# Transposing attention probabilities by 64x64 matmuls in the four quarters of the array

## The chip, the cores and the metric

The kernel runs on one core of one Trainium2 chip. Its metric is the device time of one execution in microseconds. Three runs of the kernel before took 2162.98, 2164.35 and 2164.65 us; their median is 2164.35 us.

## The reference

A layer of a graph network over 128 graphs of 64 nodes, with 512 channels, in float32: layer norm, attention with 8 heads of 64 channels inside each graph (only where `adj` allows), an output projection with a residual, a second layer norm and an MLP of width 2048 with a residual. Cut to what matters:

```python
nx = _layernorm(x, ln1_g, ln1_b)
q = (nx @ Wq + bq).reshape(B, S, HEADS, HEAD_DIM)      # B = 128 graphs, S = 64 nodes
k = (nx @ Wk + bk).reshape(B, S, HEADS, HEAD_DIM)
v = (nx @ Wv + bv).reshape(B, S, HEADS, HEAD_DIM)
scores = jnp.einsum('bqhd,bkhd->bhqk', q, k) / np.sqrt(HEAD_DIM)
scores = jnp.where(adj_mask[:, None, :, :], scores, NEG)
attn = jax.nn.softmax(scores, axis=-1)
out = jnp.einsum('bhqk,bkhd->bqhd', attn, v).reshape(B, S, H)
x = x + out @ Wo + bo
nx = _layernorm(x, ln2_g, ln2_b)
return x + jax.nn.gelu(nx @ W1 + b1, approximate=False) @ W2 + b2
```

The last product of the attention sums over the keys, so the probabilities, which come out of the softmax with the queries on the partitions, have to be turned until the keys lie there. That turn is what changes.

## The kernel before

There are 8192 tokens, that is 64 tiles of 128 tokens. A tile holds two graphs: graph a = 0 on partitions 0 to 63 and graph a = 1 on partitions 64 to 127. The attention half of the kernel goes through 16 groups of four tiles; two tiles make a pair, so each group has two pairs u = 0 and u = 1, and t = 0, 1 is the tile in its pair. The MLP half follows and is not touched.

The order of the work on TensorE in one group is a list written out by hand (`ORDER`). Its letters are steps: S the scores of a pair, P the transposition of a pair's probabilities, O the product of probabilities and values ("attend"), W the output projection of a tile, and U one of the twelve units that make queries, keys and values of the group after. The list is S0, U0 to U3, P0, U4, U5, S1, O0, U6, U7, W0, U8, W1, P1, U9, O1, U10, U11, W2, W3. Groups 1 to 12 are a hardware loop of two groups a turn; the last two groups have lists of their own (the last one has late units of the values, L, and first products of the MLP, F, between its steps). Each U and each W is twelve matmuls of 128x512 (lines 181 to 183), because a product is made of three matmuls over split parts, for four blocks of channels.

S and O already consist of 64x64 matmuls of plain float32 operands. A matmul takes rows a of the array (the partitions of its operands) and puts its result on 64 of the 128 output partitions; the innermost loops go round the four quarters. In `attend` (O, line 1361) the graph a selects the rows and also the PSUM bank, and the head's half selects the output partitions.

P is `prob_transposes` (line 1344): eight transposes of 128x128, one for each head. The stationary operand is `prob` of one head, 128 queries (two graphs) by 128 columns (two tiles by 64 keys), and the moving operand is the 128x128 identity `ident`. The result of a head has (tile t, key) on the partitions and (graph a, query) in the columns, in `ps_probT`, which is two PSUM banks of four heads each.

ScalarE then copies it to SBUF in four pieces of 64 partitions by 512 columns (`take_probT`, line 717), one for each t and a, which puts graph a on partitions 64a and up. O waits for these four copies (`probT_done`), and P waits for the softmax's last instruction on VectorE (`prob`, line 977, `prob_done`) and for the four copies of the pair before. VectorE's next `prob` in turn waits until P has read the last (`pt_done`).

Where a wait's value is held in a register, inside the loop, a helper called `wait_apart` waits and then increments a semaphore of its own that nobody waits for.

Of the kernel before, what the change touches and what calls it, by code (L numbers as in the profile page):

```python
# [31 lines left out]
F32 = mybir.dt.float32  # L32
# [6 lines left out]
P = 128  # L39
GRAPHS, NODES, HID = 128, 64, 512  # L40
HEADS = 8
# [111 lines left out]
def bank_of(g, kind, n):  # L153
    return ring_place(g, kind, n)[0]

def wait(eng, sem, value):

    if not isinstance(value, int) or value > 0:
        eng.wait_ge(sem, value)  # L160
# [10 lines left out]
def wait_apart(eng, sem, value, passed):  # L171

    wait(eng, sem, value)
    if not isinstance(value, int):
        eng.sem_inc(passed, 1)
# [9 lines left out]
def adj_layer(nc, x_dram, adj, ln1_g, ln1_b, ln2_g, ln2_b, wq, bq, wk, bk, wv, bv, wo, bo, w1, b1, w2, b2, out_dram):  # L186
# [10 lines left out]
    with ctx:  # L197
# [3 lines left out]
        def sem(name):  # L201
            return ctx.enter_context(nc.semaphore(name))
# [3 lines left out]
        ident = sb("ident", [P, P])  # L206
# [15 lines left out]
        start = nc.sbuf_base  # L222

        with ExitStack() as phase:
# [23 lines left out]
            prob = sb("prob", [P, HEADS, 2, NODES])  # L249
# [39 lines left out]
        with ExitStack() as phase:  # L289
            lin_banks = phase.enter_context(nc.psum_tensor("lin", [P, LIN, GT], F32))  # L290
            lin = [lin_banks[:, i] for i in range(LIN)]
            ps_scores = phase.enter_context(nc.psum_tensor("ps_scores", [P, HEADS, 2, NODES], F32))
            ps_probT = phase.enter_context(nc.psum_tensor("ps_probT", [P, HEADS, P], F32))
        with ExitStack() as phase:
            ps_out = [phase.enter_context(nc.psum_tensor(f"ps_out{i}", [P, HID], F32)) for i in range(TILES)]
            ps_x, ps_z, ps_y, ps_r = (phase.enter_context(nc.psum_tensor(f"ps_{n}", [P, GT], F32)) for n in "xzyr")
# [13 lines left out]
        w_loaded, w_hi_done, w_lo_done = ([sem(f"w{c}_{s}") for c in "qkvo"] for s in ("loaded", "hi_done", "lo_done"))  # L310
        cols_loaded, rows_loaded, mlp_cols_loaded = sem("cols_loaded"), sem("rows_loaded"), sem("mlp_cols_loaded")
        filled, ident_done = sem("filled"), sem("ident_done")
        s_passed, o_passed = sem("s_passed"), sem("o_passed")
        stats_done, moments_done, var_done = sem("stats_done"), sem("moments_done"), sem("var_done")
        rstd_done, zn_done, t_done = sem("rstd_done"), sem("zn_done"), sem("t_done")
        z_transposed = sem("z_transposed")
# [4 lines left out]
        prob_done, pt_done, probT_done = sem("prob_done"), sem("pt_done"), sem("probT_done")  # L321
# [345 lines left out]
        def _(act):  # L667
# [42 lines left out]
            def take_probT(g, u):  # L710

                act.wait_ge(pt_done, PAIRS * g + u + 1)
                wait(act, o_done, PAIRS * g + u)
                for t in range(2):
                    for a in range(2):
                        act.activation(probT[a * NODES:(a + 1) * NODES, t],  # L717
                                       ps_probT[t * NODES:(t + 1) * NODES, :, a * NODES:(a + 1) * NODES],
                                       ACT.Copy).then_inc(probT_done, 1)

            def att_hi(g, u):
# [5 lines left out]
            def body(g, par):  # L727
                def unit(j):
                    if "U" in kinds_of(g):
                        take = take_q if j % 3 == 0 else take_k  # L730
                        take(g + 1, 1 - par, j // 3, bank_of(g, "U", j))
                unit(0)
                exponent(g, 0)
                unit(1)
                unit(3)
                take_probT(g, 0)
                unit(4)
                if g < PREP:
                    job_hi(g, 1)
                att_hi(g, 0)  # L740
                unit(6)
                exponent(g, 1)
                unit(7)
                if g < PREP:
                    job_hi(g, 2)
                take_probT(g, 1)
                unit(9)
                att_hi(g, 1)
                unit(10)
                if "N" in kinds_of(g):  # L750
                    for k in range(KC):
                        affine(g + 2, k)
                    for k in range(KC):
                        nx_hi(g + 2, k)
                for n in ln_tiles(g):
                    ln_tile_affine(n)
# [65 lines left out]
            def last_body(g):  # L822
                for n in range(4):
                    conv_hi(0, n)
                exponent(g, 0)
                take_probT(g, 0)
                exponent(g, 1)
                att_hi(g, 0)
                snap(0, 0)
                for n in range(4, PROD):  # L830
                    conv_hi(0, n)
                take_probT(g, 1)
                att_hi(g, 1)
                snap(0, 1)
# [440 lines left out]
        def _(pe):  # L1275
# [62 lines left out]

            def prob_transposes(g, u):
                n = PAIRS * g + u  # L1340
                pe.wait_ge(prob_done, n + 1)
                wait(pe, probT_done, 4 * n)
                for h in range(HEADS):
                    mm = pe.transpose(ps_probT[:, h, :], prob[:, h, :, :], ident[:, :])  # L1344
                mm.then_inc(pt_done, 1)

            def attend(g, par, u, banks):
# [27 lines left out]
            def body(g, par):  # L1375
                for kind, n in order_of(g):
                    if kind == "S":
                        score(g, par, n)
                    elif kind == "P":
                        prob_transposes(g, n)  # L1380
                    elif kind == "F":
                        product(0, 0, n)
                    elif kind == "L":
                        unit(g, n, take_bank(g, "L", n))
                    elif kind == "U":
                        unit(g + 1, n, take_bank(g, "U", n))
                    elif kind == "O":
                        attend(g, par, n, [take_bank(g, "O", 2 * n + a) for a in range(2)])
                    elif kind == "W":
                        project(g, n, take_bank(g, "W", n))  # L1390
                    else:
                        transposes(g + 2, par, n, take_bank(g, "T", n))
# [75 lines left out]
            for t in range(TILES):  # L1468
                pe.wait_ge(zn_done, t + 1)
                for k in range(KC):  # L1470
                    mm = pe.transpose(lin[bank_of(-2, "T", k)][:, t * P:(t + 1) * P], x[0][:, t, k * P:(k + 1) * P],
                                      ident[:, :])
# [41 lines left out]
```

## Time and profile before

| what | value |
| --- | --- |
| median of three runs | 2164.35 us |
| the profiled execution, its own time | 2164.58 us |
| its span | 2162.7 us |
| TensorE busy | 2127.7 us (98%) |
| VectorE busy | 1487.9 us (69%) |
| ScalarE busy | 905.2 us (42%) |
| GpSimd busy | 433.7 us (20%) |
| mean granted TensorE clock | 0.996 |

The span is the time between the first and last instruction that the profile holds; the execution's own time is 1.9 us longer. Shares of busy time are means over stages: the attention half runs from about 60 to 855 us of the span and the MLP half from there. Times in the timeline are microseconds from the span's start. Matmuls overlap: the time that one costs is read from the start of one to the start of the next, and not from its length.

### The profile page before, as it was taken

The page shows a single profiled execution, that of the slowest core. Times are in us where ns is not written, and L with a number is a line of the kernel's source. Part 1 is how long each engine was busy: PE and PEld are TensorE (multiplying, and loading weights), DVE is VectorE, ACT ScalarE, POOL GpSimd, SP SyncE. Part 2 cuts the span into 40 slices and gives each one's busy share as a digit, 9 for nine tenths or more (in the row PEclk, how much of TensorE's full clock was granted, in tenths as well). Part 3 has the DMA queues.
Part 4 walks back from the last instruction along what each step waited for, and adds up shares of the span by engine and source line. Part 5 has one row for each costly group of instructions (what it writes and reads, how often), then busy time and mean ns, then how long its engine had stood idle before and what let it go on. Part 6 is the DMA issues. An engine that isn't in the chain of part 4 may idle for free.

```text
span 2162.7 us, 33121 instructions
## 1 busy us (share of the span) xinstructions
PE 2127.7 (98%) x13216; PEld 1756.9 (81%) x13216; DVE 1487.9 (69%) x2205; ACT 905.2 (42%) x1318; POOL 433.7 (20%) x291
## 2 busy tenths in 40 slices
PE   7999999999999988999999999999999999999999
PEld 6788888888888876888888888888888888888887
DVE  4888888888999965666666656656666666656433
ACT  3444444443344443345345345345345345345332
POOL 2333433321111114003003003003003103103200
PEclk9999999999999998999999999999999999999999
DMA  4344333331222114444544544544544544544532
GB/s 147 129 153 156 135 133 133 138 124 65 70 75 70 46 50 185 156 180 172 193 180 165 199 180 165 199 174 171 199 167 173 204 160 174 209 153 174 217 126 93
DMA packets 103793, 323.98 MB, mean 150 GB/s; under 512 B 21360, under 2 KB 29552, under 8 KB 87280
## 3 DMA queue, kind: packets, MB, share of 16 engines
q1 hardware_dynamic: 98144, 321.68, 40.4%
q8 instruction: 85, 1.39, 0.3%
q10 hardware_dynamic: 5520, 0.55, 0.2%
q14 instruction: 44, 0.36, 0.0%
HBM read 265.57 MB, written 56.62 MB: 149 GB/s over the span
## 4 chain that ended last, share of the span: by engine, by line
PE 96%; DVE 1%; ACT 1%; POOL 1%; DMA 1%; issue 0%; SPq 0%; ACTq 0%; DVEq 0%; POOLq 0%
PE lin L181 11%; PE lin L182 10%; PE lin L183 10%; PE ps_r L181 5%; PE ps_r L182 5%; PE ps_r L183 5%; PE ps_out L181 5%; PE ps_out L182 5%; PE ps_out L183 5%; PE ps_x L181 5%; PE ps_x L182 5%; PE ps_x L183 5%; PE ps_z L181 3%; PE ps_z L182 3%; PE ps_z L183 3%; PE ps_scores L1334 2%
## 5 line engine op out<-in xcount | busy, mean ns | idle before, releaser
L1168 DVE TENSOR_TENSOR acc<-ps_r,acc 128x512 f32<-128x512 f32 x256 | 176.5, 690 | 327.8 <-PE ps_r L183 327.0
L798 ACT ACTIVATE snaps<-ps_x 128x512 f32<-128x512 f32 x192 | 114.4, 596 | 410.7 <-PE ps_x L183 410.7
L181 PE MATMUL ps_r<-w_ring,h_ring 128*128 128x512 f32 x512 | 199.6, 390 | 0.9 <-DVE h_ring L1158 0.9
L181 PE MATMUL ps_x<-nxc,w_ring 128*128 128x512 f32 x512 | 199.4, 389 | 0.0
L183 PE MATMUL ps_r<-w_ring,h_ring 128*128 128x512 f32 x512 | 199.2, 389 | 0.0
L183 PE MATMUL ps_x<-nxc,w_ring 128*128 128x512 f32 x512 | 199.2, 389 | 0.0
L182 PE MATMUL ps_x<-nxc,w_ring 128*128 128x512 f32 x512 | 199.2, 389 | 0.0
L182 PE MATMUL ps_r<-w_ring,h_ring 128*128 128x512 f32 x512 | 199.2, 389 | 0.0
L181 PE MATMUL ps_out<-w_ring,h_ring 128*128 128x512 f32 x512 | 199.2, 389 | 0.0
L183 PE MATMUL ps_out<-w_ring,h_ring 128*128 128x512 f32 x512 | 199.2, 389 | 0.0
L182 PE MATMUL ps_out<-w_ring,h_ring 128*128 128x512 f32 x512 | 199.2, 389 | 0.0
L542 POOL TENSOR_TENSOR xres<-xres,bo_all 128x512 f32<-128x512 f32 x64 | 87.8, 1383 | 448.6 <-DMA xres<-in_x 444.5
L928 DVE STREAM_TRANSPOSE z1T<-x 32x512 f32<-32x512 f32 x224 | 157.5, 703 | 5.3
L928 DVE STREAM_TRANSPOSE bT<-xb 32x512 f32<-32x512 f32 x224 | 157.4, 703 | 4.3
L807 ACT ACTIVATE hf_a<-hf_a,b_cols 128x512 f32<-128x512 f32 x128 | 92.7, 724 | 150.6 <-DVE hf_a L1153 150.6
L1158 DVE TENSOR_TENSOR h_ring<-hf_b,h_ring 128x512 fp32r<-128x512 f32 x128 | 91.4, 714 | 50.3 <-ACT h_ring L814 50.1
L633 POOL TENSOR_TENSOR rstd<-var_eps,minus_half 128x4 f32<-128x4 f32 x14 | 19.4, 1384 | 500.8 <-DVE var_eps L1124 500.8
L717 ACT ACTIVATE probT<-ps_probT 64x512 f32<-64x512 f32 x128 | 75.9, 593 | 95.2 <-PE ps_probT L1344 92.8
L181 PEld LDWEIGHTS ps_r<-w_ring,h_ring 128*128 128x128 f32 x512 | 96.1, 188 | 22.5 <-issue 2.3
L697 ACT ACTIVATE qT<-lin,cols 128x512 f32<-128x512 f32 x64 | 44.1, 689 | 164.2 <-PE lin L183 164.2
L183 PEld LDWEIGHTS ps_r<-w_ring,h_ring 128*128 128x128 f32 x512 | 96.1, 188 | 20.1
L181 PEld LDWEIGHTS ps_x<-nxc,w_ring 128*128 128x128 f32 x512 | 96.1, 188 | 20.0
(131 smaller groups left out, 5131.1 us busy)
## 6 DMA issues: line engine op xcount, KB each, us to landing
w_ring<-w_scratch SPq DMA_DIRECT2D x64, 1792.0 KB, 7.3
w_ring<-w_scratch SPq DMA_DIRECT2D x64, 1024.0 KB, 7.1
xb<-x_scratch SPq DMA_DIRECT2D x22, 1024.0 KB, 10.2
xres<-in_x SPq DMA_DIRECT2D x64, 256.0 KB, 2.8
x_scratch<-xres SPq DMA_DIRECT2D x64, 256.0 KB, 2.2
x<-in_x SPq DMA_DIRECT2D x15, 1024.0 KB, 6.0
acc<-x_scratch SPq DMA_DIRECT2D x32, 256.0 KB, 2.9
out<-xb SPq DMA_DIRECT2D x32, 256.0 KB, 2.0
```

The costliest lines, as they stand in the source:

```text
L181: pe.matmul(out, lhs[1], rhs[0], start=first, stop=False, skip_group_check=resumed)
L182: pe.matmul(out, lhs[0], rhs[1], start=False, stop=False, skip_group_check=resumed)
L183: return pe.matmul(out, lhs[0], rhs[0], start=False, stop=last, skip_group_check=resumed)
L542: pool.tensor_tensor(xres[:, t % 2], xres[:, t % 2], bo_all[:, :], ALU.add).then_inc(xres_biased, 1)
L697: act.activation(qT[par][:, m, :], lin[bank][:, :], ACT.Identity, bias=cols[:, 2, m:m + 1]).then_inc(q_done, 1)
L717: act.activation(probT[a * NODES:(a + 1) * NODES, t], ps_probT[t * NODES:(t + 1) * NODES, :, a * NODES:(a + 1) * NODES], ACT.Copy).then_in ...
L798: act.activation(snaps[:, j], ps_x[:, :], ACT.Copy).then_inc(snap_done[j], 1)
L807: act.activation(hf[c], ps_x[:, :] if c == "C21" else hf[c], ACT.Gelu, bias=b1_cols[:, m:m + 1]).then_inc(gelu_done[c], 1)
L928: return dve.transpose(to[channels, :, :].rearrange("p k (t n) -> p t k n", n=P)[:, :, :, tokens], source[tokens, :, :].rearrange("p t (k ...
L1158: dve.tensor_tensor(h_ring[:, n % 2, 1, at], hf[c], h_ring[:, n % 2, 0, at].bitcast(F32), ALU.subtract).then_inc(h_split[c], 1)
L1168: dve.tensor_tensor(acc(t), ps_r[:, :], acc(t), ALU.add).then_inc(acc_added, 1)
L1334: mm = pe.matmul(ps_scores[a * NODES:(a + 1) * NODES, h * KC + m, t, :], qT[par][rows, m, at:at + NODES], kT[par][rows, m, at:at + NODES], ...
```

## The change

P becomes 32 plain matmuls of 64x64 for each pair in place of eight transposes of 128x128. For each head, tile t and graph a, the stationary operand is the 64x64 block `prob[graph a, head, tile t]`, the moving operand the 64x64 block of the identity on the same partitions, and the result goes to the output partitions of tile t. The graph selects the array's rows and the PSUM bank, the tile the array's columns. The bank of graph a now holds all eight heads of that graph side by side, so each of ScalarE's four copies reads 512 columns in a row from one bank, where it read eight runs of 64 columns, four in each of two banks. The four copies, what they write, and everything on VectorE, GpSimd and the DMA queues are as before.

The two waits ahead of P change places, and the one for `prob_done` goes through `wait_apart` with a new semaphore `p_passed`.

```diff
-            ps_probT = phase.enter_context(nc.psum_tensor("ps_probT", [P, HEADS, P], F32))
+            ps_probT = phase.enter_context(nc.psum_tensor("ps_probT", [P, 2, HEADS, NODES], F32))
...
-        s_passed, o_passed = sem("s_passed"), sem("o_passed")
+        s_passed, p_passed, o_passed = sem("s_passed"), sem("p_passed"), sem("o_passed")
...
                         act.activation(probT[a * NODES:(a + 1) * NODES, t],
-                                       ps_probT[t * NODES:(t + 1) * NODES, :, a * NODES:(a + 1) * NODES],
+                                       ps_probT[t * NODES:(t + 1) * NODES, a],
                                        ACT.Copy).then_inc(probT_done, 1)
...
                 n = PAIRS * g + u
-                pe.wait_ge(prob_done, n + 1)
                 wait(pe, probT_done, 4 * n)
+                wait_apart(pe, prob_done, n + 1, p_passed)
                 for h in range(HEADS):
-                    mm = pe.transpose(ps_probT[:, h, :], prob[:, h, :, :], ident[:, :])
+                    for t in range(2):
+                        for a in range(2):
+                            rows = slice(a * NODES, (a + 1) * NODES)
+                            mm = pe.matmul(ps_probT[t * NODES:(t + 1) * NODES, a, h, :], prob[rows, h, t, :],
+                                           ident[rows, rows], start=True, stop=True)
                 mm.then_inc(pt_done, 1)
```

On TensorE, inside the loop, P0 stands between U3 (queries' weights `wq`) and U4 (keys' weights `wk`). The rows are instructions in program order, moving operand named first; "x7" is a run of equal instructions, and names in brackets are semaphores waited for.

```order
 L182 MATMUL lin<-nxT_lo,wq_hi 128x512
 L183 MATMUL lin<-nxT_hi,wq_hi 128x512
-L1341 REGISTER_ALU
-L160 REGISTER_ALU [waits prob_done]
-L1344 MATMUL ps_probT<-ident,prob 128x128 [waits probT_done]
-L1344 MATMUL ps_probT<-ident,prob 128x128 x7
+L160 REGISTER_ALU
+L160 REGISTER_ALU [waits probT_done]
+L1347 MATMUL ps_probT<-ident,prob 64x64 [waits prob_done]
+L1347 MATMUL ps_probT<-ident,prob 64x64 x31
 L181 MATMUL lin<-nxT_hi,wk_lo 128x512 [waits q_done]
 L182 MATMUL lin<-nxT_lo,wk_hi 128x512
```

The step keeps its place; 8 matmuls become 32, and the wait on the first of them is now the one for the softmax.

P1, on the same engine in the same loop, stands between W1 (output weights `wo`) and U9, and only U9 lies between it and O1, which needs its result.

```order
 L182 MATMUL lin<-wo_lo,attT_hi 128x512
 L183 MATMUL lin<-wo_hi,attT_hi 128x512
-L1341 REGISTER_ALU
-L1344 MATMUL ps_probT<-ident,prob 128x128 [waits probT_done,prob_done]
-L1344 MATMUL ps_probT<-ident,prob 128x128 x7
+L160 REGISTER_ALU [waits probT_done]
+L1347 MATMUL ps_probT<-ident,prob 64x64 [waits prob_done]
+L1347 MATMUL ps_probT<-ident,prob 64x64 x31
 L181 MATMUL lin<-nxT_hi,wq_lo 128x512 [waits k_done]
 L182 MATMUL lin<-nxT_lo,wq_hi 128x512
```

Here too nothing moves past another step: the neighbours of P1 are the same before and now.

## Rows read from the trace of the kernel before

**Rows 1.** Head of the page: span, busy time of each engine, its share, instructions.

```profile
span 2162.7 us, 33121 instructions
PE 2127.7 (98%) x13216; PEld 1756.9 (81%) x13216; DVE 1487.9 (69%) x2205; ACT 905.2 (42%) x1318; POOL 433.7 (20%) x291
```

**Rows 2.** Busy time by stretch: length, then each engine, PEclk, DMA share, GB/s.

```profile
107.00:760.00 653.00, 652.88 (x6002) 539.49 (x5994) 563.26 (x831) 279.28 (x398) 179.60 (x139) 1.00 0.31 108
```

**Rows 3.** Timeline of TensorE: start, length, engine, line, operation, count; P1, later O1.

```profile
140.56 0.39 PE L183 MATMUL lin<-wo_hi,attT_hi 128*128 128x512 f32 x1
140.79 1.03 PE L1344 MATMUL ps_probT<-ident,prob 128*128 128x128 f32 x8
...
141.90 0.40 PE L182 MATMUL lin<-nxT_lo,wq_hi 128*128 128x512 f32 x1
...
144.18 0.39 PE L183 MATMUL lin<-nxT_hi,wq_hi 128*128 128x512 f32 x1
144.50 1.16 PE L1361 MATMUL lin<-probT,v 64*64 64x64 f32 x64
...
145.93 0.39 PE L182 MATMUL lin<-nxT_lo,wk_hi 128*128 128x512 f32 x1
```

**Rows 4.** The same timeline around S0 of a group in the loop.

```profile
206.70 0.39 PE L183 MATMUL lin<-wo_hi,attT_hi 128*128 128x512 f32 x1
207.02 1.16 PE L1334 MATMUL ps_scores<-kT,qT 64*64 64x64 f32 x64
...
208.45 0.39 PE L182 MATMUL lin<-nxT_lo,wq_hi 128*128 128x512 f32 x1
```

**Rows 5.** One line's instructions: records, ns minimum/median/maximum, starts, forms; S, O, P.

```profile
L1334 PE MATMUL ps_scores<-kT,qT x2048: 218/218/365, 54.3 to 821.1; 64*64 64x64 f32 x187
...
L1361 PE MATMUL lin<-probT,v x2048: 218/218/268, 75.7 to 848.3; 64*64 64x64 f32 x187
...
L1344 PE MATMUL ps_probT<-ident,prob x256: 270/272/477, 68.3 to 844.4; 128*128 128x128 f32 x128
```

**Rows 6.** Timeline of ScalarE's copies after P1, then O1 and its copy.

```profile
242.51 2.44 ACT L717 ACTIVATE probT<-ps_probT 64x512 f32<-64x512 f32 x4 [0.97 <-PE ps_probT L1344]
...
245.13 1.16 PE L1361 MATMUL lin<-probT,v 64*64 64x64 f32 x64
...
246.36 1.03 ACT L724 ACTIVATE attT_hi<-lin 128x1024 fp32r<-128x1024 f32 x1 [0.43 <-PE lin L1361]
```

**Rows 7.** Timeline of group 13's end: ScalarE's copy after O1, VectorE's instruction behind it.

```profile
749.82 1.03 ACT L724 ACTIVATE attT_hi<-lin 128x1024 fp32r<-128x1024 f32 x1 [0.43 <-PE lin L1361]
...
750.98 1.23 DVE L984 TENSOR_TENSOR attT_lo<-lin,attT_hi 128x1024 fp32r<-128x1024 f32 x1
```

**Rows 8.** Timeline of TensorE behind its two longest waits in the last two groups.

```profile
774.25 1.97 PE L1344 MATMUL ps_probT<-ident,prob 128*128 128x128 f32 x8 [3.91 <-DVE prob L977]
...
776.44 0.63 PE L182 MATMUL lin<-nxT_lo,wk_hi 128*128 128x512 f32 x1
...
819.41 1.99 PE L1334 MATMUL ps_scores<-kT,qT 64*64 64x64 f32 x64 [7.08 <-DVE softmax L958]
...
821.92 0.63 PE L182 MATMUL lin<-wv_lo,nxT_hi 128*128 128x512 f32 x1
```

**Rows 9.** Timeline of the last group: P0 and ScalarE's copies of it.

```profile
828.57 1.03 PE L1344 MATMUL ps_probT<-ident,prob 128*128 128x128 f32 x8
...
829.64 2.45 ACT L717 ACTIVATE probT<-ps_probT 64x512 f32<-64x512 f32 x4 [6.67 <-PE ps_probT L1344]
```

**Rows 10.** Timeline of TensorE: S1 and O0 back to back, the slowest in the loop.

```profile
426.99 1.16 PE L1334 MATMUL ps_scores<-kT,qT 64*64 64x64 f32 x64
428.19 1.16 PE L1361 MATMUL lin<-probT,v 64*64 64x64 f32 x64
```

**Rows 11.** Costliest groups on the page: two ScalarE copies out of PSUM.

```profile
L798 ACT ACTIVATE snaps<-ps_x 128x512 f32<-128x512 f32 x192 | 114.4, 596 | 410.7 <-PE ps_x L183 410.7
...
L717 ACT ACTIVATE probT<-ps_probT 64x512 f32<-64x512 f32 x128 | 75.9, 593 | 95.2 <-PE ps_probT L1344 92.8
```

## Prediction

> **What bounds the kernel now.** I read the page's engine totals first, then busy time by stretch, then the timeline of TensorE around the changed step. The totals put TensorE at 98% of the span and VectorE at 69% [rows 1]; the reader should see that only TensorE is near its limit, but a share alone says nothing about one stage. The stretch does: from 107 to 760 us, which is the steady part of the attention half, TensorE is busy for 652.88 of 653.00 us, at the full granted clock (1.00, the 2.4 GHz level) [rows 2]. It waits for nobody there. So in this stretch a step is worth what it takes on TensorE, both ways, and what the other engines do is cover. Only in the last two groups do the long waits stand, 3.91 us for the softmax and 7.08 us ahead of the last scores [rows 8].
>
> Since matmuls overlap, I price a step from the last matmul ahead of it to the second one behind it, so that a late start, the stream itself and a slow first matmul behind it are all inside.
>
> **The price of P now.** From the matmul at 140.56 to the second one behind P1 at 141.90 is 1.34 us, eight transposes included [rows 3].
>
> **The price of P then.** No transposition by quarters is in this trace, but two steps have its shape: S and O are each 32 written matmuls of 64x64x64 in float32, going round the four quarters, and in O the graph picks the array's rows and the bank, just as it will in P. Around O1 the same distance is 144.18 to 145.93, 1.75 us [rows 3], and around S0 it is 206.70 to 208.45, again 1.75 us [rows 4]. All S and O in the stretch that stand alone between 128-row matmuls read the same within 0.01 us, but for the one or two that rows 10 stand for. So a P will cost 1.75 - 1.34 = 0.41 us more.
>
> Why eight full transposes are cheaper than 32 quarter products is also to be read: O and S have 2048 records each for 32 pairs, that is 64 a step, so a written float32 product becomes two passes; P has 256, eight a step, one for each transpose [rows 5]. The work per step goes from 8 records to 64.
>
> The Trainium skill, "TensorE: Matmul & The Clock Gate" (Terms, at xbus), says that transpose mode is four times as fast for FP32, and "TensorEngine Tiling (Array Packing)" (Feature Incompatibilities) that column tiling excludes that mode for such input. By these rules P goes from 8 x 128 columns to 32 x 64 x 4 / 4 quarters = 2048, and the 1024 more cost 0.43 us at 2.4 GHz; by the rows it is 0.41. The trace agrees in size, though it shows two records a product and not four; the sum would be 13.3 us by the pages' figure and 12.8 by the rows.
>
> **The sum.** There are 32 P steps.
> - 29 of them lie where TensorE is continuously fed (both of groups 0 to 12, P0 of group 13, P1 of groups 14 and 15): 29 x 0.41 = 11.9 us. For group 14 that holds because O1 behind it feeds ScalarE and GpSimd work on which the 7.08 us wait ends.
> - P1 of group 13 runs while VectorE is the late engine. It still delays O1 and so ScalarE's copy, which ends at 750.85, 0.13 us before VectorE takes it up [rows 7]. 0.41 less 0.13 is about 0.3 us, bounded by 0 and 0.41.
> - P0 of group 14 starts when the softmax releases it and runs at the half clock (lengths of 0.63 where 0.39 is usual). From its start to the second matmul behind it is 776.44 - 774.25 = 2.19 us, and for the S step in the same condition 821.92 - 819.41 = 2.51 us [rows 8]: 0.3 us more.
> - P0 of the last group releases the copies on which the exponent, the softmax and the next projection hang. The copies start 1.07 us after P starts [rows 9]; behind an O a copy starts 1.23 us after (245.13 to 246.36) [rows 6]. A quarter step also starts 0.09 us later (0.32 against 0.23 from the matmul ahead) [rows 3]. That is 0.25 us.
>
> Together 11.9 + 0.3 + 0.3 + 0.25 = 12.8 us. On the profiled execution's 2164.58 us that makes 2177.4; this execution lies 0.2 us above the median of the three runs, so I predict 2177.2 us.
>
> **Edits costed at nothing.** ScalarE's copies: reading 512 columns in a row takes 596 ns where eight runs of 64 take 593 [rows 11], so four copies change by some 0.01 us, and TensorE covers them. Does O1 now wait for them? The four end at 244.95 and O1 starts at 245.13, a slack of 0.18 us [rows 6], with U9 alone between P1 and O1. With quarters the copies are released 0.25 us later (1.23 - 1.07 + 0.09), while U9 and O1 come 0.41 us later, so the slack grows by 0.16 us; if it did not hold, each of the 16 O1 steps would wait by the shortfall. The exchange of the two waits: the late one of the two, the softmax, now stands on the first matmul; in the stretch TensorE waits for neither, so their order can't show, and behind both are the same twelve matmuls of a unit. `p_passed` adds an increment that S and O have too, inside the 1.75 us. The softmax's next `prob` waits for P's end, which comes 0.25 us later, but VectorE's queue is also shifted by TensorE; nothing is late there.
>
> **Bounds of the unknown price.** Towards cheap: S0 and O0 of a pair back to back keep a stream without leaving the quarters; were P to lose its late start and its slow exit (0.09 and 0.03 us), it would cost 0.29 us, and the sum 9 us. Towards dear: the slowest pair in the loop has 428.19 - 426.99 = 1.20 us between two steps [rows 10], 0.1 to 0.15 us over the rest, which I read as a late instruction fetch; if every P had it, 32 x 0.15 = 4.8 us come on top, 2182. I take the common value, since 0.41 repeats in nearly every row of the same form.
>
> **Rivals.**
> 1. *The quarters run four at once and P gets shorter.* Eight transposes start some (1.03 - 0.27) / 7 = 0.108 us apart [rows 3, 5]; a 64-column product would take half of it, and four side by side make 8 rounds of 0.054, 0.43 us where 0.87 stood: 32 x 0.43 = 14 us gained, 2150 us. Against it stands that S and O already go round the four quarters and take 1.75 us; no row is faster. 3%.
> 2. *A product with the identity goes through in one pass, as the transposes do.* Then 32 records in place of 64. In O records start (1.16 - 0.218) / 63 = 15 ns apart [rows 3, 5]; 32 fewer save 0.48 us, so P would be 0.07 us shorter than now: 32 x 0.07 = 2 us gained, 2162 us, no change that can be told. Against it: the number of records goes with the operands' type in S and O, and that is the same here. 5%.
> 3. *Hidden.* If TensorE were not the bound in the attention half, the 0.41 us would vanish in waits: 2165 us. Against it: 0.12 us of idle time in 653 [rows 2]. 3%.
> 4. *Slower still.* The loop's program grows, and each P pays the late fetch of rows 10, or O1 does come to wait for the copies: 2179 to 2183 us. 9%.
>
> **Numbers.** The forecast has 80%, with 2174 to 2180 as its own range. A change within 0.2% (4.3 us) can't be told from none by a measurement of this kernel. Faster gets rival 1 and part of rival 2, 5%; the same gets the rest of 2, rival 3 and a P priced at a third of the difference, 6%; slower 89%. The range from 2171 to 2183 us takes in both bounds of the price and rival 4.
>
> **What would show it.** In the profile after, P should have 2048 records of 64x64, the distance across a P should be 1.75 us where 1.34 stood, and the MLP half should start some 13 us later and take as long as before. TensorE should still be busy all through the steady stretch, and O1 should start 0.32 us behind its neighbour, with no wait for the copies. I am wrong if P has 1024 records, if the distance is under 1.5 us, or if TensorE's idle time in the steady stretch rises above a few microseconds.

## The result and the profile after

The changed kernel takes 2174.02 us (median of six runs, 2173.23 to 2176.39) against 2163.35 us for the kernel before (six runs, 2161.71 to 2164.65). The ratio is 1.0051 with a 95% interval of 1.0038 to 1.0064: it is slower, by 10.7 us, and the interval allows 8 to 14, which takes in the forecast 12.8. Its profiled execution took 2174.2 us with a span of 2172.4 us.

The page's head, to be read beside [rows 1], shows that only TensorE got more to do: 11.0 us more busy time in 1792 more matmul records, which is 32 steps times 56. The other engines have as many instructions as before.

```profile
span 2172.4 us, 36717 instructions
PE 2138.7 (98%) x15008; PEld 1758.2 (81%) x15008; DVE 1490.3 (69%) x2205; ACT 906.8 (42%) x1318; POOL 432.5 (20%) x291
```

The timeline of TensorE around P1 of the same group as in [rows 3] (start, length, operation, count):

```profile
140.96 0.39 PE L183 MATMUL lin<-wo_hi,attT_hi 128*128 128x512 f32 x1
141.28 1.16 PE L1347 MATMUL ps_probT<-ident,prob 64*64 64x64 f32 x64
142.37 0.50 PE L181 MATMUL lin<-nxT_hi,wq_lo 128*128 128x512 f32 x1
142.71 0.39 PE L182 MATMUL lin<-nxT_lo,wq_hi 128*128 128x512 f32 x1
```

From 140.96 to 142.71 is 1.75 us where 1.34 stood, with 64 records in it. All its fed P steps read the same within 0.02 us, and in the loop so does every O and S standing alone, but for the first scores in three of its six turns, which start late by 0.05 to 0.3 us. The records of the line, beside [rows 5]:

```profile
L1347 PE MATMUL ps_probT<-ident,prob x2048: 218/218/267, 67.4 to 854.1; 64*64 64x64 f32 x187
```

And the steady stretch, beside [rows 2] (its columns are the same), in which TensorE still waits for almost nothing:

```profile
107.00:765.00 658.00, 657.65 (x7430) 537.46 (x7422) 559.33 (x818) 274.41 (x390) 178.15 (x139) 1.00 0.32 107
```

### The profile page after: what moved, and what is told of

Read it like the earlier page. It is cut to its first block, busy times and chain, and to the rows that moved or that the text cites. A ratio compares the mean times of both kernels' runs of the same rounds, so it can differ in the third digit from the quotient of the medians.

```text
span 2172.4 us, 36717 instructions
## 1 busy us (share of the span) xinstructions
PE 2138.7 (98%) x15008; PEld 1758.2 (81%) x15008; DVE 1490.3 (69%) x2205; ACT 906.8 (42%) x1318; POOL 432.5 (20%) x291
## 4 chain that ended last, share of the span: by engine, by line
PE 95%; DVE 1%; DMA 1%; ACT 1%; POOL 1%; issue 0%; SPq 0%; ACTq 0%; DVEq 0%; POOLq 0%
PE lin L181 11%; PE lin L182 10%; PE lin L183 10%; PE ps_r L181 5%; PE ps_r L183 5%; PE ps_r L182 5%; PE ps_x L181 5%; PE ps_x L183 5%; PE ps_out L183 5%; PE ps_x L182 5%; PE ps_out L182 5%; PE ps_out L181 5%; PE ps_z L183 3%; PE ps_z L182 3%; PE ps_z L181 3%; PE ps_probT L1347 2%
## 5 line engine op out<-in xcount | busy, mean ns | idle before, releaser
L717 ACT ACTIVATE probT<-ps_probT 64x512 f32<-64x512 f32 x128 | 76.1, 595 | 101.4 <-PE ps_probT L1347 99.1
L181 PEld LDWEIGHTS ps_r<-w_ring,h_ring 128*128 128x128 f32 x512 | 96.1, 188 | 22.6 <-issue 2.1
L182 PEld LDWEIGHTS ps_out<-w_ring,h_ring 128*128 128x128 f32 x512 | 96.1, 188 | 20.0
```

Of the source, the lines that this page charges most:

```text
L181: pe.matmul(out, lhs[1], rhs[0], start=first, stop=False, skip_group_check=resumed)
L182: pe.matmul(out, lhs[0], rhs[1], start=False, stop=False, skip_group_check=resumed)
L717: act.activation(probT[a * NODES:(a + 1) * NODES, t], ps_probT[t * NODES:(t + 1) * NODES, a], ACT.Copy).then_inc(probT_done, 1)
```

## The experiments

P's price is given throughout as in the prediction: from the last matmul ahead of it to the second one behind. "Stream" is from P's first record to the next step's, divided by P's records. Both are medians over the steps that TensorE is fed for.

| kernel | records in a P | stream of one, ns | P across, us | time against before |
| --- | --- | --- | --- | --- |
| before: 8 transposes, full array | 8 | 99 | 1.34 | |
| changed: 32 plain products, quarters in turn | 64 | 17 | 1.75 | 1.0051 [1.0038, 1.0064] |
| e1: the exchanged waits alone | 8 | 99 | 1.34 | 1.0000 [0.9991, 1.0010] |
| e2: 8 plain products, full array | 16 | 106 | 2.24 | 1.0143 [1.0128, 1.0159] |
| e3: quarters in bfloat16 | 32 | 11.7 | 1.03 | 1.0011 [1.0002, 1.0020] |
| e4: 16 transposes, row halves | 16 | 40 | 1.30 | 1.0013 [1.0004, 1.0022] |
| e5: e4 with 192 instructions ahead of the loop | 16 | 40 | 1.30 | 0.9993 [0.9984, 1.0002] |
| e9: the changed kernel, one quarter after another | 64 | 52 | 3.99 | 1.0398 [1.0380, 1.0415] |
| e10: 16 plain products, row halves | 32 | 60 | 2.59 | 2217.24 us, one run |

**e1: the waits without the matmuls.**

```diff
-                pe.wait_ge(prob_done, n + 1)
                 wait(pe, probT_done, 4 * n)
+                wait_apart(pe, prob_done, n + 1, p_passed)
```

> The kernel before with the two waits exchanged and the increment of p_passed, transposes and PSUM layout as before. Theory A (the price is in the matmuls alone): P stays at 1.34 us from the matmul ahead to the second behind, the time is that of the kernel before within 2 us. Rival B (the separate wait stops weights from being loaded ahead, or the increment holds TensorE's sequencer): P starts 0.32 us after its neighbour in place of 0.23, up to 0.1 us more for each P, 3 us in all.

Theory A: 2162.77 us against 2163.12. The step still starts 0.23 us behind its neighbour, and its second follower at 90.45 is 1.33 us behind 89.12:

```profile
89.12 0.39 PE L183 MATMUL lin<-wo_hi,attT_hi 128*128 128x512 f32 x1
89.35 1.03 PE L1344 MATMUL ps_probT<-ident,prob 128*128 128x128 f32 x8
90.14 0.48 PE L181 MATMUL lin<-nxT_hi,wq_lo 128*128 128x512 f32 x1
90.45 0.39 PE L182 MATMUL lin<-nxT_lo,wq_hi 128*128 128x512 f32 x1
```

So the whole price is in the matmuls.

**e2: plain products without quarters.**

```diff
-                    mm = pe.transpose(ps_probT[:, h, :], prob[:, h, :, :], ident[:, :])
+                    mm = pe.matmul(ps_probT[:, h, :], prob[:, h, :, :], ident[:, :], start=True, stop=True)
```

> The kernel before with each transpose of 128x128 replaced by a plain float32 matmul with the identity, full array, waits and layout as before. Theory A (two passes of a plain float32 product are the price, and the four quarters give a part of it back): P has 16 records and takes more than the quarters' 1.75 us, estimated from a half-speed pass (16 x 0.108 us and more) at 2.2 to 2.6 us, so 27 to 40 us over the kernel before. Rival B (the price of the change is going in and out of the quarters): no quarters, no price, P at 1.34 us and the time of the kernel before.

Theory A: 16 records, 2.24 us across, 2195.11 us. The rival, that a way in and out of the quarters is the price, falls as the main cause: without quarters P costs 0.49 us more than with them.

```profile
89.82 0.39 PE L183 MATMUL lin<-wo_hi,attT_hi 128*128 128x512 f32 x1
90.04 1.95 PE L1344 MATMUL ps_probT<-ident,prob 128*128 128x128 f32 x16
91.75 0.48 PE L181 MATMUL lin<-nxT_hi,wq_lo 128*128 128x512 f32 x1
92.06 0.40 PE L182 MATMUL lin<-nxT_lo,wq_hi 128*128 128x512 f32 x1
```

A record takes 106 ns here and 99 ns as a transpose: a plain float32 product shows as two records, two passes, each about as long as the one pass of a transpose. The 0.90 us on 32 steps make 29 of the 32 us; most of the rest is in waits that the page puts down to issue, 3.8 us in all, at the same place in five turns of the loop.

**e3: the quarters with one pass.** The probabilities are rounded to bfloat16 here, and so is the identity.

```diff
-            prob = sb("prob", [P, HEADS, 2, NODES])
+            prob = sb("prob", [P, HEADS, 2, NODES], mybir.dt.bfloat16)
...
-                                           ident[rows, rows], start=True, stop=True)
+                                           ident_r[rows, rows], start=True, stop=True)
```

> The changed kernel with the probabilities and the identity of P in bfloat16, so that a quarter product is one pass; this rounds the probabilities. Theory A (passes): 32 records for each P in place of 64, at 15 to 17 ns each, so P takes 1.2 to 1.25 us where the changed kernel has 1.75 and the kernel before 1.34: 3 to 5 us faster than before, 14 to 17 faster than the changed kernel. Rival B (a fixed cost of 32 small matmuls or of the quarters, whatever their passes): P stays near 1.75 us, 10 us over before.

```profile
88.77 0.39 PE L183 MATMUL lin<-wo_hi,attT_hi 128*128 128x512 f32 x1
89.09 0.45 PE L1351 MATMUL ps_probT<-ident_r,prob 64*64 64x64 bf16 x32
89.46 0.50 PE L181 MATMUL lin<-nxT_hi,wq_lo 128*128 128x512 f32 x1
89.80 0.39 PE L182 MATMUL lin<-nxT_lo,wq_hi 128*128 128x512 f32 x1
```

On P theory A holds with room: 32 records, 1.03 us, 0.31 us less than the eight transposes. (bfloat16 halves the passes and the width of the operands at once, so that the passes alone make the difference is not shown by this run.) On the time both theories missed: 2166.04 us, 2.9 us over before, where 32 x 0.31 should have saved 10. The first of the loop's six turns has the gain, 99.53 us from the matmul ahead of its first scores to that of the next turn, where the kernel before takes 100.65; the five behind it take 101.4 to 103.8. The missing part begins in the first scores of these turns:

```profile
204.13 0.80 PE L1338 MATMUL ps_scores<-kT,qT 64*64 64x64 f32 x36
206.56 0.68 PE L1338 MATMUL ps_scores<-kT,qT 64*64 64x64 f32 x28 [1.63 <-issue]
```

TensorE stops in the middle of a run of 64 equal records and waits for nothing that the profile shows of another engine. Against the first turn the five lose 16.1 us in this profile. Idle time at this place is 9.6 us of it; behind three of the five stops the granted clock also fell to 0.50 for 3.4 us, so the next matmuls ran at the lower level and cost about 1.5 us more each time. One such stretch, in the columns of [rows 2], read 0.1 us off the fall on either side:

```profile
310.20:313.60 3.40, 3.40 (x10) 2.65 (x9) 3.33 (x4) 0.00 (x0) 0.00 (x0) 0.51 1.07 372
```

**e4: transposes in row halves.** One transpose for each head and graph: 64 rows of the array, all 128 columns.

```diff
                 for h in range(HEADS):
-                    for t in range(2):
-                        for a in range(2):
-                            rows = slice(a * NODES, (a + 1) * NODES)
-                            mm = pe.matmul(ps_probT[t * NODES:(t + 1) * NODES, a, h, :], prob[rows, h, t, :],
-                                           ident[rows, rows], start=True, stop=True)
+                    for a in range(2):
+                        rows = slice(a * NODES, (a + 1) * NODES)
+                        mm = pe.transpose(ps_probT[:, a, h, :], prob[rows, h, :, :], ident[rows, rows])
```

> The changed kernel's layout, with two transposes for each head, each of one graph: 64 rows of the array and all 128 columns, so the one-pass transpose stays and the two halves lie in different banks; 16 records for each P. Theory A (loading 128 columns and streaming 64 columns is what a transpose takes, and the two row halves run side by side): 16 x (128 + 64) / 2 columns are 0.64 us where 8 x 256 are 0.85, with 0.12 us for entering and leaving the halves, so P takes about 1.25 us and the kernel is some 3 us faster than before. Rival B (the halves do not run side by side): 1.28 us of stream, P about 1.85 us, 16 us slower than before.

```profile
88.81 0.39 PE L183 MATMUL lin<-wo_hi,attT_hi 128*128 128x512 f32 x1
89.13 0.71 PE L1346 MATMUL ps_probT<-ident,prob 64*128 64x64 f32 x16
89.77 0.50 PE L181 MATMUL lin<-nxT_hi,wq_lo 128*128 128x512 f32 x1
90.10 0.39 PE L182 MATMUL lin<-nxT_lo,wq_hi 128*128 128x512 f32 x1
```

P's stream is 0.64 us as theory A had it, and 1.29 us across in these rows. The kernel is slower all the same, 2165.93 against 2163.12, because the five turns of the loop behind the first again lose about 1 us each (101.4 to 101.9 us where the first takes 100.53), here at the fourth matmul of U0 (208.36, where 0.23 us behind 207.10 was due):

```profile
205.44 1.16 PE L1334 MATMUL ps_scores<-kT,qT 64*64 64x64 f32 x64
...
207.10 0.40 PE L183 MATMUL lin<-nxT_hi,wq_hi 128*128 128x512 f32 x1
208.36 0.49 PE L181 MATMUL lin<-nxT_hi,wq_lo 128*128 128x512 f32 x1 [0.86 <-issue]
```

**e5 and e6: the place of the loop in the program.** The two P steps ahead of the loop grow by 32 instructions (a weight load and a matmul for each record) in e2 and e4, by 96 in e3, by 224 in the changed kernel. The stall's place moves to match: 32 instructions more put it behind the third matmul of U0, 96 put it 28 records and those three matmuls earlier. If a new piece of the program has to arrive at a fixed spacing, which the expectations below put at 256 instructions, then the place can be shifted at will with matmuls that do nothing, run while TensorE waits for the first tiles:

```diff
             pe.wait_ge(ident_done, 1)
+            for _ in range(48):        # 16 in e6
+                pe.matmul(lin[0][0:1, 0:1], ident[:, 0:1], ident[:, 0:1], start=True, stop=True)
```

> The halves kernel with 48 float32 matmuls of one column ahead of everything on TensorE, while it waits for the first tiles; each is two passes of a weight load and a matmul, 192 instructions, which move the program of the loop on by 192 instructions and change nothing else. Theory A (the stalls that the page puts down to issue, 0.5 to 1.0 us at the fourth matmul of U0 in each turn of the loop, come from where the loop's first instruction lies in a fetched piece of 256 instructions): they vanish, and with P at 1.30 us where the kernel before has 1.34 the time is 1 to 2 us below before. Rival B (they come from the halves themselves, or from the size of the loop): they stay at 3.5 us in all and the time stays some 2 us above before.

> The changed kernel with 16 such matmuls ahead, 64 instructions. Theory A (the place of the loop in the fetched pieces): the changed kernel has 224 instructions more ahead of the loop than the kernel before and the halves 32 more; with 64 more still it is at 288, which is 32 over a piece of 256, so the stall appears at the fourth matmul of U0 in each of five turns, 0.5 to 1.0 us each, and the kernel is 2.5 to 5 us slower than the changed one, 2177 to 2179 us. Rival B: no new stall, the changed kernel's time of 2174 within 1.5 us.

Theory A in both. In e5 the stalls are gone (658.00 of 658.00 us busy from 107 to 765 us) and the time is 2161.82 against 2163.77 us; the gain of the halves, 0.04 us a step or 1.3 us in all, shows at about its due size, though the interval, 0.9984 to 1.0002, does not exclude none. In e6 the changed kernel, which had no such stall, got it at the very instruction that was named:

```profile
208.98 1.16 PE L1334 MATMUL ps_scores<-kT,qT 64*64 64x64 f32 x64
...
210.64 0.40 PE L183 MATMUL lin<-nxT_hi,wq_hi 128*128 128x512 f32 x1
211.69 0.50 PE L181 MATMUL lin<-nxT_hi,wq_lo 128*128 128x512 f32 x1 [0.65 <-issue]
```

It took 2179.73 us, 1.0078 of before [1.0062, 1.0093]: 16.0 us over the kernel before, where the changed kernel is 10.7 over, so some 5.3 us more; I had said 2.5 to 5. In the profile the five turns lose 5.0 us against the first. The idle time shown (0.65) undercounts the delay (1.05 less the usual 0.23), since the end of a matmul overlaps it.

One more thing in these traces speaks for a late arrival. In e2, e3, e4, e6 and e10 every stop ends 2.4 to 3.1 us after the first score of its turn, whether 36 or 67 records stand ahead of it. With 0 or 224 instructions more, the same place of the program would lie 166 or 198 instructions into the turn, by the spacing of 256; the kernel before and the changed one get there 5.5 and 9.2 us after the first score, and do not stop.

**e7 and e8: which groups pay.** e7 has the quarters in groups 0 to 12 alone, e8 in groups 13 to 15 alone; the other groups keep the transposes.

```diff
+def quarters(g):
+    return not (isinstance(g, int) and g >= NG - 3)      # e8: without the "not"
...
+                if quarters(g):
                     for h in range(HEADS):      # the 32 products
...
+                else:
+                    for h in range(HEADS):
+                        mm = pe.transpose(ps_probT_old[:, h, :], prob[:, h, :, :], ident[:, :])
```

> Quarters in groups 0 to 12 alone, 26 of the 32 P steps; the last three groups keep the eight transposes and their layout. Theory A (in the fed part each P costs 0.41 us, and in the last three groups the sum of the prediction, 2.1 us, is lost because the wait for the softmax in group 14 hangs on a DMA and TensorE's clock then stays up or not): 10.7 us over before, so no faster than the changed kernel, 2173 to 2175. Rival B (the last three groups cost what the sum says): 2.1 us less than the changed kernel, about 2172.

> Quarters in groups 13 to 15 alone, 6 of the 32 P steps. Theory A: between 0 and 1 us over before. Rival B: 2.1 us over before, the wait for the softmax in group 14 as long as before and the clock behind it at the half level as before.

e7 took 2174.07 us, as much as the changed kernel with 26 of its 32 steps. That is theory A's time, but its interval, 1.0033 to 1.0064 or 7 to 14 us over before, holds rival B's 8 to 9 too, so it decides nothing. e8 took 2166.7 us, 1.0014 of before [1.0005, 1.0024], 1 to 5 us: rival B's 2.1 is inside it and theory A's 1 just at its end, and in its profile the wait was 4.54 us and the granted clock behind it 0.50, as rival B had it. The extra times of the two, 10.3 and 2.9 us, come to 13.2: nearer to the forecast 12.8 than to the 10.7 of the whole change, with intervals that allow either. The stretches of the profiled executions, from start to start of P steps, show where executions differ:

| kernel | P0 of group 0 to P1 of 13 | P1 of 13 to P0 of 14 | P0 of 14 to P1 of 15 |
| --- | --- | --- | --- |
| before | 676.60 | 29.38 | 69.39 |
| e1 | 677.17 | 28.93 | 69.69 |
| changed | 688.41 | 28.29 | 68.97 |
| e6 | 692.81 | 28.47 | 70.25 |
| e7 | 687.46 | 28.19 | 69.58 |
| e8 | 677.45 | 30.33 | 70.25 |

The first column carries the change, +11.8, +10.9 and +0.9 us for 27, 26 and one quarter steps in the changed kernel, e7 and e8; e1, with none, has +0.6, so that much is the spread of executions (e6 has its stops besides). The second moves by 2 us with no regard to what P is. In the third, e6 and e8, with quarters, take 0.6 to 0.9 us more than before, e1 and e7, with transposes, where the terms of the sum had about 1 us due; only the changed kernel's own profile takes less than before.

**e9: one quarter after another.** The same 32 products, the loop over heads innermost.

```diff
-                for h in range(HEADS):
-                    for t in range(2):
-                        for a in range(2):
+                for t in range(2):
+                    for a in range(2):
+                        for h in range(HEADS):
                             rows = slice(a * NODES, (a + 1) * NODES)
```

> The changed kernel with the same 32 products of P in another order: all eight heads in one quarter, then the next quarter. Theory A (the quarters work side by side, and a P of 64 records at 17 ns depends on it): in one quarter records follow one another at 27 ns (64 columns) to 53 ns (64 loaded and 64 streamed) at the full clock, so P takes 2.4 to 4.1 us in place of 1.75, 20 to 75 us over the changed kernel. Rival B (17 ns is what the sequencer needs to issue a record, and no quarter runs beside another): P stays at 1.75 us and the time at 2174.

2249.77 us; P's 64 records take 3.33 us, 52 ns each, against 17 in turn:

```profile
66.71 0.39 PE L183 MATMUL lin<-nxT_hi,wq_hi 128*128 128x512 f32 x1
67.03 3.40 PE L1347 MATMUL ps_probT<-ident,prob 64*64 64x64 f32 x64
70.36 0.50 PE L181 MATMUL lin<-nxT_hi,wk_lo 128*128 128x512 f32 x1
70.70 0.40 PE L182 MATMUL lin<-nxT_lo,wk_hi 128*128 128x512 f32 x1
```

Theory A, at the dear end. The time is 86.2 us over before, 75.5 more than the changed kernel's 10.7, at the end of the range too. The quarters do work side by side: taking turns is 3.1 times as fast as staying in one.

**e10: plain products in row halves.** e4 with `pe.matmul(..., start=True, stop=True)` in place of `pe.transpose`.

> The halves kernel with plain float32 matmuls in place of the transposes. Theory A (a plain float32 product is two passes, each a load of 128 columns and a stream of 64, two row halves side by side): 32 records at 40 ns, 1.28 us from P's first matmul to the next step where the halves with transposes have 0.64, P about 1.94 us, some 20 us over the halves kernel. Rival B (the passes cost less where the array is split): under 1.7 us for P.

The step is dearer than either said: 60 ns a record, 2.59 us across, 2217.24 us in its one run. Doubling the passes here takes not twice but three times the stream (1.93 against 0.64 us). Five turns of its loop also stop where e3's do, for 9.3 us in all, and the granted clock falls to 0.50 behind three of these stops.

```profile
90.42 0.39 PE L183 MATMUL lin<-wo_hi,attT_hi 128*128 128x512 f32 x1
90.74 2.00 PE L1346 MATMUL ps_probT<-ident,prob 64*128 64x64 f32 x32
92.67 0.50 PE L181 MATMUL lin<-nxT_hi,wq_lo 128*128 128x512 f32 x1
93.01 0.39 PE L182 MATMUL lin<-nxT_lo,wq_hi 128*128 128x512 f32 x1
```

## Why the prediction was right, point by point

**The bound and the price.** TensorE was the bound and stayed it, and each fed P costs 0.41 us more, as S and O had shown. The table lets the price be reckoned as a sum. These records by themselves take about the time of their loaded and streamed columns, one after the other, at 2.4 GHz: 128 and 128 are 107 ns (measured 99 to 106), 64 and 64 are 53 ns (52 in e9). Side by side, four quarters would make 13.3 ns of the latter, two halves of 128 and 64 would make 40 (40 in e4). This is a reckoning and no floor: e3's 11.7 ns and the transposes' 99 lie below it, and the 128x512 matmuls around P start 0.23 us apart, where 128 and 512 columns would be 0.27. By it a P of 64 passes in quarters would take 64 x 13.3 = 0.85 us, just what eight passes of a full transpose would take, 8 x 107 = 0.85: smaller tiles and twice the passes cancel. What is left is the price: 0.12 us for going into the quarters and out of them, seen also in e4, and 17 instead of 13.3 ns a record, 0.24 us; the transposes, at 99 ns, are another 0.06 us under their reckoning. That records of one product, two passes in the same quarter, follow each other and hinder the overlap would explain the 17, the 60 ns of e10 and the 11.7 of e3, which has single passes; no experiment here set the passes of one product apart, so this part is argued and not shown. The prediction's other working, 1024 more columns for 0.43 us, came near by luck: it has 0.43 us for the eight transposes and 0.85 us for the products, whose streams take 0.79 and 1.09 us.

**The sum.** 12.8 us were predicted for 10.7, and the interval of 8 to 14 holds both, so the 2.1 us between them are not clear of noise. In the two profiles, 9.7 us apart, the parts are:
- Ahead of P1 of group 13, 27 steps: 27 x 0.41 = 11.1 us due, 11.8 found; the first scores of three loop turns start late, 0.5 us in all, where the kernel before loses 0.3 in two places. The 0.7 us between is about what e1 shows with no change in its matmuls.
- P1 of group 13: 0.3 due. VectorE's `attT_lo` moved from 750.98 [rows 7] to 762.18, while that P1 moved from 744.87 to 755.85: 11.20 - 10.98 = 0.22 us.
- P0 of group 14 is the term that came out otherwise: 0.3 us more were due, and together with the wait ahead of it 2.1 us less came. The softmax came 9.81 us later than before although VectorE's work ahead of it came 11.2 us later, because between them VectorE waits for a layer-norm tile (`spare`) which SyncE's queue fetches in order, and the queue had been held up before. VectorE's timeline, before and after:

```profile
770.42 0.69 DVE L1061 BATCH_NORM_STATS2 a_stats<-spare 128x6 f32<-128x512 f32 x1 [3.97 <-DMA spare<-x_scratch]
```

```profile
780.22 0.69 DVE L1061 BATCH_NORM_STATS2 a_stats<-spare 128x6 f32<-128x512 f32 x1 [2.57 <-DMA spare<-x_scratch]
```

  Queue of DMA issues before and after (start, length, transfer):

```profile
763.09 1.40 SPq L370 DMA_DIRECT2D mask<-in_adj  x1
765.60 0.99 SPq L375 DMA_DIRECT2D xres<-in_x  x2
766.68 0.85 SPq L407 DMA_DIRECT2D spare<-x_scratch  x2
```

```profile
774.30 0.46 SPq L370 DMA_DIRECT2D mask<-in_adj  x1
775.36 1.05 SPq L375 DMA_DIRECT2D xres<-in_x  x2
776.51 0.85 SPq L407 DMA_DIRECT2D spare<-x_scratch  x2
```

  Issuing the mask took 1.40 us before, 0.46 after, 0.46 in e7 and 1.79 in e8. TensorE's wait was 2.50 us long instead of 3.91, and this time its clock did not fall: the granted clock is 1.00 from 783 to 790 us, where it was 0.50 from 773.8 to 777.0 before, around the first of [rows 8]. So P0 and its followers ran at full speed:

```profile
784.14 1.16 PE L1347 MATMUL ps_probT<-ident,prob 64*64 64x64 f32 x64 [2.50 <-DVE prob L977]
785.24 0.50 PE L181 MATMUL lin<-nxT_hi,wk_lo 128*128 128x512 f32 x1
785.57 0.39 PE L182 MATMUL lin<-nxT_lo,wk_hi 128*128 128x512 f32 x1
```

  From its start to the second matmul behind it is now 1.43 us, against 2.19 with transposes at the half clock. I had carried the wait and the clock of the one profile over as if they belonged to the program. But the term itself was sized right for the case that it named: in e6 and e8, where the clock did fall, the same step takes the 2.51 us that the prediction read from S. Timeline of e6:

```profile
789.03 1.99 PE L1347 MATMUL ps_probT<-ident,prob 64*64 64x64 f32 x64 [2.68 <-DVE prob L977]
...
791.54 0.63 PE L182 MATMUL lin<-nxT_lo,wk_hi 128*128 128x512 f32 x1
```

  Of the twelve kernels' profiles the changed kernel's is the only one in which the clock did not fall at or just behind this step; the median of six runs does not tell how many of them had that luck. Why that issue takes 0.5 or 1.4 to 1.8 us is open; the SyncE program is the same in all of these, and in e1 it was the issue ahead of it, `x_scratch<-xres`, that took longer (2.09 us for the two, 0.92 before and after).
- P0 of the last group: the copies start 1.23 us behind P's start (839.03 against 837.80), as taken from O. From there to P1 it takes 15.31 us where it took 15.07: 0.24 us, for 0.25 due.

The start of the profile before was also late: its first P stands at 68.27 us, at 67.44 in the one after, at 66.9 to 67.2 in e1 to e4 and again at 68.28 in e5. That takes 0.8 us off the span's difference, and no term explains it. With it and the 2.1 us of group 14, P1 of the last group, and the MLP half behind it, starts only 9.5 us later than before, where some 13 had been named; from that P1 to the end both profiles take the same, 1319.1 and 1319.25 us.

**Edits at nothing.** The exchange of the waits costs nothing (e1). O1's slack against the copies was to grow by 0.16 from 0.18 us: the copies now end at 247.65, O1 starts at 248.01, 0.36 us.

```profile
245.20 2.45 ACT L717 ACTIVATE probT<-ps_probT 64x512 f32<-64x512 f32 x4 [2.20 <-PE ps_probT L1347]
...
248.01 1.16 PE L1365 MATMUL lin<-probT,v 64*64 64x64 f32 x64
```

**The rivals.** "Four at once" is half true: the quarters do overlap (e9), and in one pass a P of quarters beats the transposes by 0.31 us (e3). It fails here because a float32 product has two passes. "One pass" is refuted by the 2048 records; its price was also too small, since a pass saved in e3 was worth 0.72 us a P and not 0.48: P's records there follow each other at 11.7 ns and not at the 15 that were read from lengths, whose ends are modelled. (In the same way the 108 ns of the transposes in rival 1 are 99 from start to start, and the steps back to back in the bounds are S1 and O0, as in [rows 10].) "Hidden" is refuted by the steady stretch, 0.35 us idle in 658. "Slower still" did not happen, but only by the luck of 224 instructions: with 64 more the kernel is at 2179.7 us (e6), by a stop in each of five turns and not by a delay of each P.

## What to carry to other kernels

Before a transpose is turned into small matmuls, count passes times columns: a float32 transpose is one pass and a float32 matmul two, which eats what quarters of the array give back; row halves keep the transpose's single pass and gave a P of 1.30 against 1.34 us, too little to show clear of noise in the time (e5). A term read from one profile's wait and clock may belong to that execution alone: look for it in a second profile. Price a new step from a step of the same shape that the trace already has, between the same neighbours. And when a change moves instructions ahead of a hardware loop, look at the first hundred or so records of each turn: a time that gets worse by some microseconds may be where the loop lies in the program, and that can be moved.

## What the runs showed of the hardware

- A turn of the loop, from the second on, can leave TensorE idle for 0.3 to 2.2 us at a place that is fixed in the program: behind about 134 instructions of the loop when 32 or 288 more stand ahead of it (e2, e4, e6), behind about 72 when 96 more do (e3 and e10). These places agree with a period of 256 instructions; one of 128 would have put a stop behind about 70 with 224 more, where the changed kernel, e5, e7 and e9 have none. That it is the arrival of the next piece of program, asked for when the loop jumps back, I infer from this, from the stops' all ending 2.4 to 3.1 us into the turn and from there being no other releaser; the fetch itself was not seen.
- In one quarter 64 float32 records of 64x64 take 52 ns each, in turn over four quarters 17 ns, in bfloat16 11.7 ns.
- TensorE waits 2.3 to 4.5 us for the softmax ahead of P0 of group 14 in all twelve profiles. In eleven its granted clock fell to 0.50, for 3.4 us or more, at some moment from 0.5 us before P's start to 1.4 after; in the changed kernel's, behind 2.50 us, it stayed at 1.00. It fell behind shorter waits too (2.34 us in e9, 2.29 in e10), so the length of the wait alone does not say whether it falls. Where it falls before P, the step and its two followers take 2.17 to 2.19 us in place of 1.11 with transposes and 2.51 in place of 1.43 with quarters.
